# Sixteen-head attention stage: order of the SyncE queue, place of the reciprocals, and width of the high and low parts of the scaled sums

## The reference

```python
y = x.reshape(b, t, nh, hs).transpose(0, 2, 1, 3)            # nh = 16, hs = 8
scores = jnp.einsum('bhtk,bhsk->bhts', y, y) / math.sqrt(hs)
attn = jax.nn.softmax(scores, axis=-1)
o = jnp.einsum('bhts,bsc->bhtc', attn, x)
o = o.transpose(0, 2, 1, 3).reshape(b, t, nh * c)
return o @ weight                                            # added to x
```

## Time and profile before

| | us |
|---|---|
| time of the kernel before, median of 3 runs | 2703.54 |
| lowest and highest of the 3 | 2698.01, 2705.41 |
| the profiled execution | 2697.12 |
| its span in the trace | 2695.3 |
| head stage: first scores of head 0, last scores matmul of head 63 (starts) | 645.6, 1628.3 |

### The profile page before, as it was taken

One profiled execution on the slowest core, in us unless ns is written; L12 is line 12 of the kernel. 1 busy time (PEld: TensorE's weight loads), 2 busy tenths in 40 slices (PEclk: granted clock), 3 DMA queues, 4 the chain that ended last, 5 costly groups with the idle time before them and its releaser, 6 DMA issues. The chain is left out here.

```text
span 2695.3 us, 34921 instructions
## 1 busy us (share of the span) xinstructions
PE 2519.3 (93%) x11075; PEld 1901.4 (71%) x11075; DVE 2166.5 (80%) x2872; ACT 1826.3 (68%) x3038; POOL 1213.5 (45%) x1258
## 2 busy tenths in 40 slices
PE   7899999996999999999999998899999999788888
PEld 4788888874666666666666665688888886567656
DVE  6677777776999999999989996777777776578665
ACT  4455555556888888888888985455555555657676
POOL 3566666664223323233223222366666664154401
PEclk9999999998999999999999998999999999888899
DMA  4566666645333333333333331566666660000001
GB/s 111 115 143 141 137 137 138 145 97 167 100 107 101 101 109 102 103 104 100 104 102 101 101 104 34 116 137 142 142 145 144 142 142 9 24 24 9 9 3 37
DMA packets 107384, 271.46 MB, mean 101 GB/s; under 512 B 30784, under 2 KB 35648, under 8 KB 107072
## 3 DMA queue, kind: packets, MB, share of 16 engines
q1 hardware_dynamic: 82192, 235.42, 35.1%
q0 software_dynamic: 24576, 33.62, 4.5%
q10 hardware_dynamic: 432, 0.20, 0.0%
HBM read 258.35 MB, written 10.76 MB: 100 GB/s over the span
## 5 line engine op out<-in xcount | busy, mean ns | idle before, releaser
L684 POOL TENSOR_TENSOR moe_experts_lo<-moe_experts_hidden,moe_experts_hi 128x512 fp32r<-128x512 f32 x512 | 661.0, 1291 | 341.6 <-ACT moe_experts_hi L622 341.5
L962 DVE TENSOR_TENSOR heads_e_lo<-heads_e,heads_e_hi 128x2048 fp32r<-128x2048 f32 x256 | 585.5, 2287 | 54.9 <-ACT heads_e_hi L910 52.3
L629 ACT ACTIVATE psum<-psum 128x512 f32<-128x512 f32 x512 | 298.0, 582 | 478.9 <-PE psum L90 478.9
L797 POOL DMA_DIRECT2D heads_left<-heads_parts x512 | 296.1, 600 | 678.5 <-PE psum L851 613.8
L903 ACT ACTIVATE heads_e<-psum 128x1024 f32<-128x1024 f32 x512 | 520.1, 1023 | 104.0 <-PE psum L851 104.0
L656 DVE TENSOR_TENSOR moe_experts_weighted<-moe_spread,psum 128x512 f32<-128x512 f32 x512 | 350.8, 685 | 189.8 <-PE psum L90 185.8
L88 PE MATMUL psum<-heads_e_hi,heads_v_lo 128*128 128x512 f32 x1024 | 425.3, 415 | 1.4 <-DVE heads_u L929 1.4
L88 PE MATMUL psum<-moe_n_hi,moe_w_lo 128*128 128x512 f32 x1024 | 400.8, 391 | 5.8 <-PEq L54 5.7
L89 PE MATMUL psum<-heads_e_lo,heads_v_hi 128*128 128x512 f32 x1024 | 402.5, 393 | 0.0
L90 PE MATMUL psum<-heads_e_hi,heads_v_hi 128*128 128x512 f32 x1024 | 401.2, 392 | 0.0
L89 PE MATMUL psum<-moe_n_lo,moe_w_hi 128*128 128x512 f32 x1024 | 399.8, 390 | 0.0
(11 more groups left out here) (403 smaller groups left out, 4057.2 us busy)
## 6 DMA issues: line engine op xcount, KB each, us to landing
moe_spread<-moe_mask SPq DMA_DIRECT2D x128, 1024.0 KB, 10.1
heads_right<-heads_parts SPq DMA_DIRECT2D x512, 64.0 KB
heads_left<-heads_parts POOLq DMA_DIRECT2D x512, 64.0 KB, 2.7
heads_scale<-heads_inverse_copy SPq DMA_DIRECT2D x64, 512.0 KB, 3.6
moe_experts_raw<-in_gate SPq DMA_DIRECT2D x16, 256.0 KB, 11.6
moe_experts_raw<-in_up SPq DMA_DIRECT2D x16, 256.0 KB, 11.6
moe_experts_raw<-in_down SPq DMA_DIRECT2D x16, 256.0 KB, 11.6
heads_parts<-heads_e_hi SPq DMA_DIRECT2D x16, 256.0 KB, 3.2
```

The costliest lines, as they stand in the source:

```text
L629: act.activation(psum[:, GATE + p % 2, :], psum[:, GATE + p % 2, :], ACT.Silu).then_inc(silu_ready, 1)
L684: pool.tensor_tensor(lo[:, p, :], hidden[:, p % 2, :], f(hi[:, p, :]), ALU.subtract).then_inc(low_ready, 1)
L797: eng.dma_start(f(tile[row:row + 2 * HEAD, h % 2, :]), parts_dram[dims, order:order + 2, at]).then_inc(loaded[h % 2], 16)
L962: dve.tensor_tensor(e_lo[:, s:s + 2, :], e[:, s % 4:s % 4 + 2, :], f(e_hi[:, s:s + 2, :]), ALU.subtract).then_inc(low, 1)
```

## The change

Four edits in `head_attention`:

1. On SP the wait for the scores of head h and the eight loads of `right` for head h + 2 move from the end of iteration h to its front, ahead of the wait for the reciprocals, the stores and the scale load.
2. `invert(h)` moves on DVE from behind the high part of tile 0 of head h + 1 to behind the low parts of tiles 6 and 7 of head h, ahead of `u_lows(h - 1)`; the extra call after the loop goes.
3. The high part of `u` (ACT) and its low part (DVE) become single instructions of 1024 columns. `scale_sums` stays at two instructions, each counted by `scaled_ready`; the high part now waits for both.
4. The wait of `scale_sums(g)` for the low parts of the head before stands once ahead of both multiplications, and counts one per head.

```diff
                 for h in range(COUNT):
+                    if h + 2 < COUNT:
+                        sp.wait_ge(scores_done, (h + 1) * TILES)
+                        load_head(sp, right, (0, 1), h + 2, right_loaded)
                     sp.wait_ge(inverse_ready, h + 1)
...
                     sp.dma_start(scale[:, h % 2, :], inverse_dram[h % 2:h % 2 + 1, :].to_broadcast([P, T])
                                  ).then_inc(scale_loaded[h % 2], 16)
-                    if h + 2 < COUNT:
-                        sp.wait_ge(scores_done, (h + 1) * TILES)
-                        load_head(sp, right, (0, 1), h + 2, right_loaded)
...
-                    pe.wait_ge(u_low, (g + 1) * HALVES)
+                    pe.wait_ge(u_low, g + 1)
...
                 def u_highs(g):
                     after(act, sum_done, g - 1)
-                    for half in range(HALVES):
-                        act.wait_ge(scaled_ready, g * HALVES + half + 1)
-                        act.copy(u_hi[:, g % 2, half, :], u[:, half, :]).then_inc(u_high, 1)
+                    act.wait_ge(scaled_ready, (g + 1) * HALVES)
+                    act.copy(u_hi[:, g % 2, :], u[:, :]).then_inc(u_high, 1)
...
                     dve.wait_ge(out_done, (g + 1) * TILES)
+                    after(dve, u_low, g)
                     for half in range(HALVES):
-                        after(dve, u_low, (g - 1) * HALVES + half + 1)
...
                 def u_lows(g):
-                    for half in range(HALVES):
-                        dve.wait_ge(u_high, g * HALVES + half + 1)
-                        dve.tensor_tensor(u_lo[:, g % 2, half, :], u[:, half, :], f(u_hi[:, g % 2, half, :]),
-                                          ALU.subtract).then_inc(u_low, 1)
+                    dve.wait_ge(u_high, g + 1)
+                    dve.tensor_tensor(u_lo[:, g % 2, :], u[:, :], f(u_hi[:, g % 2, :]), ALU.subtract).then_inc(u_low, 1)
...
-                    if s == 0 and h >= 1:
-                        invert(h - 1)
...
+                    if s == TILES - 2:
+                        invert(h)
                     if s == TILES - 2 and h >= 1:
                         u_lows(h - 1)
...
-                invert(COUNT - 1)
                 scale_sums(COUNT - 1)
```

More of the change, by code:

```diff
@@ L763, in head_attention @@
         scale = sb(f"{tag}_scale", [P, 2, T])
-        u = sb(f"{tag}_u", [P, HALVES, BANK])
-        u_hi, u_lo = sb(f"{tag}_u_hi", [P, 2, HALVES, BANK], F32R), sb(f"{tag}_u_lo", [P, 2, HALVES, BANK], F32R)
+        u = sb(f"{tag}_u", [P, T])
+        u_hi, u_lo = sb(f"{tag}_u_hi", [P, 2, T], F32R), sb(f"{tag}_u_lo", [P, 2, T], F32R)
         SCORES, OUT, SUM = 0, 4, 6
@@ L835, in add_head @@
                     for half in range(HALVES):
+                        at = slice(half * BANK, (half + 1) * BANK)
                         last = product(pe, psum[:, SUM + half, :], (w_hi[:, cols], w_lo[:, cols]),
-                                       (u_hi[:, g % 2, half, :], u_lo[:, g % 2, half, :]),
+                                       (u_hi[:, g % 2, at], u_lo[:, g % 2, at]),
                                        first=g % HEADS == 0, last=g % HEADS == HEADS - 1)
@@ L926, in scale_sums @@
                     dve.wait_ge(out_done, (g + 1) * TILES)
+                    after(dve, u_low, g)
                     for half in range(HALVES):
-                        after(dve, u_low, (g - 1) * HALVES + half + 1)
-                        dve.tensor_tensor(u[:, half, :], scale[:, g % 2, half * BANK:(half + 1) * BANK],
-                                          psum[:, OUT + half, :], ALU.mult).then_inc(scaled_ready, 1)
+                        at = slice(half * BANK, (half + 1) * BANK)
+                        dve.tensor_tensor(u[:, at], scale[:, g % 2, at], psum[:, OUT + half, :], ALU.mult).then_inc(scaled_ready, 1)
                 def u_lows(g):
-                    for half in range(HALVES):
-                        dve.wait_ge(u_high, g * HALVES + half + 1)
-                        dve.tensor_tensor(u_lo[:, g % 2, half, :], u[:, half, :], f(u_hi[:, g % 2, half, :]),
-                                          ALU.subtract).then_inc(u_low, 1)
+                    dve.wait_ge(u_high, g + 1)
+                    dve.tensor_tensor(u_lo[:, g % 2, :], u[:, :], f(u_hi[:, g % 2, :]), ALU.subtract).then_inc(u_low, 1)
                 def add_batch(b):
```

## The result

The changed kernel took 2676.62 us (median of 4 runs, 2671.88 to 2681.52) against 2704.26 us (4 runs): ratio 0.9903, interval 0.9879 to 0.9926. Timed once more on another occasion it was 0.9884 (0.9862 to 0.9906). The forecast was 2676.

A forecast was written before the change was run, and what follows sets the result against it. PE's 15.02 us per head was taken as floor, with late right operand loads stalling it above that. Terms -26.8 - 0.9 + 0 = -27.7 us took the profiled 2697.12 to 2669.4; plus 6.4 for the median, 2676, range 2667 to 2688.

The forecast's parts named there:

- PE's floor and the 31 stalls: Head stage: PE needs 15.02 us per head; 31 waits before the scores, for late right operand loads, all go: -26.8 us.
- More than 10 us to spare.: Right operand loads on SP, issued 10.5 us earlier, would be ready more than 10 us before the scores need them.
- `invert` earlier, -0.9 us: Reciprocals on DVE 1.75 us earlier, so the scale load lands earlier and PE's waits for `heads_u` shrink by 0.9 of 1.4 us.
- the scale load 2.18 us later as now: On SP the scale load would still go out 2.18 us after the stores' first issue, landing at 1222.3 instead of 1224.0.
- the plain sum: Stores and scale load follow the earlier reciprocals without waiting for operand bursts; whole change -26.8 - 0.9 + 0 = -27.7 us.
- the rule: Stores' completion waits for both operands' earlier writes; scale load lands at 1224.3, about as today: 0.9 us lost, 26.8 kept.
- Single instructions: High and low parts of `u`: 0 in the stage; tail +0.9 us, offset by earlier reciprocals (-1.1 at most), so 0.
- Rival A (DVE): Head stage: DVE sets the pace once the stalls go, 15.2 us per head, 12 us lost, 2688; chance 0.06.
- Rival C (scale path): Stores and scale load held behind both bursts, PE stands before `weighted_rows`: 18 us net slower, 2722; chance 0.03.
- Rivals B and D: B: right operand stays partly late, half the stalls stay, 2689; D: stalls have another cause, 2703; chance 0.03 each.
- some us on either side: Stages behind the heads: granted clock varies as they start some 28 us earlier, so the range was widened both ways.

The follow-up runs named there:

- the copies: The whole change plus one or two DVE copies of 1024 columns per head into an unread buffer: stage of heads 2 to 63 at 918 us with one, 939.0 with two.

## Why the prediction was right, and where not

- *PE's floor and the 31 stalls.* Right, in size too: 26.8 us reckoned. In the stage 25.4 us went in the first profile (944.07 - 918.64) and 26.5 in the second (944.07 - 917.59); the head layer as a whole gave 26.7. That the right operand was what PE waited for is shown twice by the runs: two different edits that bring its loads forward each remove the stalls (one all, the other all but two or three), and the edit that leaves its loads alone leaves 31. The trace of the kernel before says the same: in 31 of the last 61 heads the scores start 0.09 us behind the last increment of the right operand's semaphore, and in the changed kernel the shortest distance is 8.7 us.
- *"More than 10 us to spare."* Nearly: it was 9.6 us in the median, since beside the other burst the right operand's last load landed 4.8 us after its issue. It also shows what the prediction left out: 1.75 us would have done in nearly every head, so edit 2, credited with 0.9 us at most, was worth 24 by itself.
- *`invert` earlier, -0.9 us.* Wrong, and this is the step that failed: "the scale load 2.18 us later as now". The stores did go out 1.75 us earlier (17.2 us into the head), but the scale load at 21.3 instead of 19.4: it follows the landing of the bursts, which the plain sum did not have in the path. The working under the rule, with both bursts ahead of the stores, had put it about where it was before, with the 0.9 us lost and the 26.8 kept. The place of the scale load came out so. Of the 0.9 us less can be said: PE's waits for `heads_u` are 1.5 us in one profile of the changed kernel and 0.2 in the other, so a term of this size is within what differs between two executions. I had taken the plain sum and kept the rule for a bound; with the reciprocals reckoned 0.5 us behind the end of the right loads' issue, the other order of trust was the better one.
- *Single instructions.* Worth 0 in the stage, right. In the tail +0.9 was reckoned and 0.95 measured; the earlier reciprocals gave their part back. From the first scores of head 63 to PE's first matmul behind the wait it was 27.07 us before and 27.08 after: 0, as forecast.
- *Rival A (DVE).* It did not come. The prediction's 0.8 us of idle time was nearly right: the copies put DVE's work at 14.3 of 15.03 us.
- *Rival C (scale path).* Its mechanism is there, its size is not: the scale load stays within PE's 1.1 us of slack, apart from at most three heads in 64.
- *Rivals B and D.* They did not come: no wait before the scores is left.
- *The total.* 2676.6 against 2676 is closer than the parts deserve. The profile fell short of its own sum (2669.4) by 12.1 us, 10.8 of which are the last layers at a lower granted clock; they are the "some us on either side" of the range. That the medians agree to 0.6 us is luck: on the second occasion the changed kernel's median was 2671.72 us.

## What to carry to other kernels

When an engine's stalls are shorter than a microsecond or two, any step of the loop that feeds them may cure them, and the cures do not add: ask for each edit what it is worth once the others are made, and alone. When loads are moved ahead of a small store on whose completion something waits, count that completion from the landing of what is in flight, other queues' loads included, and not from the store's issue (here 0.8 us behind the landing, whether the stores were issued 17.2 or 18.4 us after the head's start). Judge such a change by the stage that it touches: two profiles of the same kernel differed by 1 us in the stage and by 13 us in the total.

## What the runs showed of the hardware

- Four stores of 1 KB on the SP queue were waited for 0.84 to 0.96 us per head with no burst around them or one nearly landed, 1.7 us with loads of the POOL queue in flight beside them, and 2.45 to 2.55 us behind two bursts of 512 KB. From 0.96 to 1.7 it is the start of POOL's loads alone that differs (61.7 against 109.0 us in 64, the same eight loads ahead on SP). It agrees with what the Trainium skill says in "DMA: Bandwidth & Descriptors", section "Queues, rings and completion order", that a completion waits for the DMA engine's earlier writes across its queues. These runs do not separate that from the mere sharing of the engines' time, nor, behind two bursts, from order within the SP queue.
- The 64 KB loads on the POOL queue landed 3.8 us after issue in the median when the right operand's burst ran beside them, and 2.7 before.
- One DVE subtraction of 1024 columns took 1184 ns in this stage, against 1223 ns in the last attention.
- A DVE copy of 1024 columns between two instructions of which the second reads what the first wrote cost 0.48 us, not its 0.6 from start to start: the pair's own starts were 0.72 us apart, and 1.20 with the copy between them.
